# A graph network on one core: target look-ups, both moves of the edge order and its high digit placed inside the attention stages

## The reference, cut to what matters

```python
h = jnp.maximum(_layernorm(x, axis=-1), 0.0)
x = x + _L0_gnn_ref(h, edge_index, edge_attr_16, ...)      # two gat_conv layers
h = jnp.maximum(_layernorm(x, axis=-1), 0.0)
x = x + _L1_gnn_ref(h, edge_weight, src, dst, 3)           # three hops over the edges
h = jnp.maximum(_layernorm(x, axis=-1), 0.0)
x = x + _L2_gnn_ref(h, edge_index, edge_attr_64, ...)      # messages
h = jnp.maximum(_layernorm(x, axis=-1), 0.0)
x = x + _L3_gnn_ref(h, edge_index, ...)                    # three convolution layers

def gat_conv(x, src, dst, edge_attr, W, ...):
    xh = (x @ W).reshape(N, H, C)                          # H = 4 heads of C = 32
    alpha = leaky_relu(a_src[src_f] + a_dst[dst_f] + a_edge, 0.2)
    p = jnp.exp(alpha - segment_max(alpha, dst_f)[dst_f])
    alpha = p / (segment_sum(p, dst_f)[dst_f] + 1e-16)
    return segment_sum(xh[src_f] * alpha[..., None], dst_f).reshape(N, H * C) + bias
```

## Time and profile before

| | us |
|---|---|
| three runs | 8554.72, 8569.4, 8579.12 |
| median of these | 8569.4 |
| the profiled execution, whole | 8508.76 |
| its span, first to last instruction | 8507.1 |
| mean granted TensorE clock, share of full | 0.699 |

### The profile page before, as it was taken

The page is one execution under the profiler, slowest core; times in us unless marked ns, Lnnn a source line. Parts: engine busy times, 40 slices in busy tenths (PEclk is TensorE's granted clock), DMA queues, the critical chain, the costliest instruction groups (busy, mean ns, idle before and its releaser), DMA issues. The chain is left out here.

```text
span 8507.1 us, 77896 instructions
## 1 busy us (share of the span) xinstructions
PE 3708.8 (44%) x17298; PEld 2510.9 (30%) x17298; DVE 4381.7 (52%) x16544; ACT 2807.7 (33%) x6612; POOL 3976.6 (47%) x4025
## 2 busy tenths in 40 slices
PE   1501116711133452000676767466657889333333
PEld 1300004401022441000343434344434555223222
DVE  6340007906041741478888979567653445444322
ACT  3800006700031221012566656344433555222111
POOL 0047771062737026334534344466655442566566
PEclk9755558955565666555788889788777778666665
DMA  1000004521033253165334333344332332555433
GB/s 46 3 18 15 17 17 156 191 92 41 15 100 91 78 212 90 27 229 185 95 92 98 98 90 99 120 145 145 136 105 79 99 98 91 182 172 174 132 107 94
DMA packets 463932, 866.81 MB, mean 102 GB/s; under 512 B 110119, under 2 KB 119700, under 8 KB 461932
## 3 DMA queue, kind: packets, MB, share of 16 engines
q1 hardware_dynamic: 349035, 681.67, 23.2%
q0 software_dynamic: 114560, 181.50, 9.5%
HBM read 415.76 MB, written 459.09 MB: 103 GB/s over the span
## 5 line engine op out<-in xcount | busy, mean ns | idle before, releaser
L2756 POOL DMA_INDIRECT gcn_ring<-GT,gcn_index x588 | 590.8, 1005 | 255.0 <-issue 171.3
L1605 POOL DMA_INDIRECT light_ring<-C,light_s_u x392 | 392.2, 1001 | 402.8 <-DVE light_acc L1648 297.5
L1499 PE MATMUL tail_psT<-ident,tail_h 128*128 128x128 f32 x784 | 142.5, 311 | 724.5 <-ACT tail_h L1448 671.5
L2857 DVE SCALAR_TENSOR_TENSOR gcn_acc<-gcn_acc,cont,gcn_ring 128x128 f32<-128x128 f32 x588 | 204.7, 348 | 371.6 <-DMA gcn_ring<-GT,gcn_index 133.8
L532 POOL DMA_INDIRECT got_s<-TAB,src_u x196 | 185.8, 948 | 429.5 <-POOLq L560 366.0
L2366 POOL DMA_INDIRECT msg_ps<-PS,msg_s_u x196 | 189.8, 969 | 354.8 <-PE msg_ps_z L2662 298.1
L1499 PEld LDWEIGHTS tail_psT<-ident,tail_h 128*128 128x128 f32 x784 | 101.2, 155 | 857.3 <-ACT tail_h L1448 750.7
L2939 PE MATMUL gcn_psA<-ident,gcn_h 128*128 128x128 f32 x588 | 132.1, 365 | 498.0 <-DVE gcn_h L2860 253.1
L1448 ACT ACTIVATE tail_h<-tail_x,tail_nmr,tail_std 128x128 f32<-128x128 f32 x784 | 320.6, 483 | 14.4 <-DVE tail_nmr L1379 7.3
L2906 ACT ACTIVATE gcn_hT<-gcn_psA 128x512 f32<-128x512 f32 x147 | 88.6, 603 | 638.4 <-DMA X3D<-msg_x 245.9
L539 POOL DMA_INDIRECT J<-sort_items,sort_place x196 | 191.1, 975 | 199.1 <-POOLq L1714 137.0
(11 more groups left out here) (615 smaller groups left out, 14266.2 us busy)
## 6 DMA issues: line engine op xcount, KB each, us to landing
T<-front_a_t SPq DMA_DIRECT2D x160, 272.0 KB
source_rows_c<-C SPq DMA_DIRECT2D x156, 256.0 KB
GT<-source_rows_r SPq DMA_DIRECT2D x156, 256.0 KB
C<-light_acc SPq DMA_DIRECT2D x147, 256.0 KB
gcn_own<-GT SPq DMA_DIRECT2D x147, 256.0 KB
RC<-gcn_own SPq DMA_DIRECT2D x147, 256.0 KB
gat_rows_r<-RG SPq DMA_DIRECT2D x104, 264.0 KB
RG<-gat_rows SPq DMA_DIRECT2D x2, 12936.0 KB
```

Of the source, the lines that this page charges most:

```text
L1499: last = nc.tensor.transpose(ps["T"][:, j * P:(j + 1) * P], rows_[:, j, :], net.ident[:, :])
L1605: nc.gpsimd.indirect_dma_start(out=ring[:, n % RING, j, :], out_offset=None, in_=tables[h], in_offset=bass.IndirectOffsetOnAxis(ap=index[: ...
L2756: nc.gpsimd.indirect_dma_start(out=ring[:, n % RING, j, :], out_offset=None, in_=net.GT[i], in_offset=bass.IndirectOffsetOnAxis(ap=index[: ...
L2857: nc.vector.scalar_tensor_tensor(out=acc[:, n % 2, j, :], in0=before, scalar=net.cont[:, c:c + 1], in1=ring[:, n % RING, j, :], op0=ALU.mu ...
```

## The change

What GpSimd does beside the front is cut up and laid beside other phases:

- The front is one block of 98 groups. GpSimd beside it fetches the target rows (`fetch_target_rows`: 196 gathers in 14 batches; GpSimd itself issues the store of each batch to XD, one batch later, and waits for a store's landing before it fills that half of the ring again) and then makes the 196 look-ups `got_s`.
- The T1 rows are gathered by source straight into Y, 196 DMAs with no ring, no waits and no copies. Y is 136 wide now, and the store to RG takes the first 132 of each row.
- The attention stage of layer 1 gets, ahead of `fix_pool`, two casts of `got_s` and the first 150 `got_d` look-ups.
- `phase_gat1_rows` gets the other 46 look-ups, the 196 scatters into J1 and the load of the items; `gat_own` goes from GpSimd to DVE.
- `phase_high_digit` follows with 28 half batches instead of 14, and GpSimd gathers T2 beside it, straight into the second Y.
- The attention stage of layer 2 has no gather and no copies; GpSimd makes 100 of the scatters into J2 there.
- In `phase_gat2_rows` GpSimd's stream is written out; after each of the first 12 iterations it issues 8 of the remaining 96 scatters, after the last one the load. The two short phases on source segments come after it.

```diff
+def fetch_target_rows(nc, net, pool, table, index, ring, arrived, stored):
+    rows = net.XD.rearrange("(p t) d -> p t d", t=T)
+    def store(k):
+        pool.wait_ge(arrived[k % 2], 16 * U * (k // 2 + 1))
+        pool.dma_start(rows[:, k * U:(k + 1) * U, :], ring[:, k % 2, :, :]).then_inc(stored[k % 2], 16)
+    for k in range(NB):
+        if k >= 2:
+            pool.wait_ge(stored[k % 2], 16 * (k // 2))
+        for u in range(U):
+            c = k * U + u
+            nc.gpsimd.indirect_dma_start(out=ring[:, k % 2, u, :], out_offset=None, in_=table,
+                                         in_offset=bass.IndirectOffsetOnAxis(ap=index[:, c:c + 1], axis=0)).then_inc(arrived[k % 2], 16)
+        if k >= 1:
+            store(k - 1)
+    store(NB - 1)
+    for half in range(2):
+        pool.wait_ge(stored[half], 16 * (NB // 2))
...
+            def fetch_and_look_up(pool):
+                fetch_target_rows(nc, net, pool, inp["x"], dst_u, xd_ring, xd_arrived, xd_stored)
+                gather_static(nc, net.TAB, src_u, got_s, looked_s)
+                pool.wait_ge(looked_s, 16 * T)
+            phase_front(nc, net, inp, "front", 0, NODE_GROUPS, fetch_and_look_up)
...
+            Y = sb("gat1_rows", [P, T, WA])
+            def fetch_sources(pool):
+                gather_static(nc, net.T1, src_u, Y, rows1_in)
+                pool.wait_ge(rows1_in, 16 * T)
+            phase_own_projection(nc, net, fetch_sources)
+            def look_up(pool):
+                nc.gpsimd.tensor_copy(packed[:, :, 3], got_s[:, :, 0]).then_inc(filled, 1)
+                nc.gpsimd.tensor_copy(q_u[:, :], got_s[:, :, 0]).then_inc(filled, 1)
+                gather_static(nc, net.TAB, dst_u, got_d, looked_d, range(LOOKUPS_BEFORE_ENDS))
+            phase_attend(nc, net, 0, Y, look_up)
         def look_up_and_move(pool):
-            gather_static(nc, net.TAB, src_u, got_s, looked_s)
-            gather_static(nc, net.TAB, dst_u, got_d, looked_d)
-            pool.wait_ge(looked_s, 16 * T)
-            nc.gpsimd.tensor_copy(packed[:, :, 3], got_s[:, :, 0]).then_inc(filled, 1)
+            gather_static(nc, net.TAB, dst_u, got_d, looked_d, range(LOOKUPS_BEFORE_ENDS, T))
             pool.wait_ge(looked_d, 16 * T)
             nc.gpsimd.tensor_copy(packed[:, :, 4], got_d[:, :, 1]).then_inc(filled, 1)
-            pool.wait_ge(filled, 2)
+            pool.wait_ge(filled, 3)
             scatter_static(nc, net.J1, place, packed, moved)
...
-        phase_front(nc, net, inp, "front_a", 0, FRONT_BESIDE_LOOKUPS, look_up_and_move)
+        phase_gat1_rows(nc, net, look_up_and_move)
...
-            phase_high_digit(nc, net, items, place, lambda pool: gather_columns(nc, pool, inp["x"], net.dst_idx, xb), store_xd)
-        phase_front(nc, net, inp, "front_b", FRONT_BESIDE_LOOKUPS, NODE_GROUPS - FRONT_BESIDE_LOOKUPS, order_edges)
+            def fetch_rows(pool):
+                gather_static(nc, net.T2, q_u, Y, rows2_in)
+                pool.wait_ge(rows2_in, 16 * T)
+            phase_high_digit(nc, net, items, place, fetch_rows)
+            phase_attend(nc, net, 1, Y, lambda pool: scatter_static(nc, net.J2, place, items, moved2, range(MOVES_BEFORE_ENDS)))
+        def move(pool, it):
+            each = -(-(T - MOVES_BEFORE_ENDS) // EDGE_ITERS)
+            scatter_static(nc, net.J2, place, items, moved2, range(MOVES_BEFORE_ENDS + it * each, min(MOVES_BEFORE_ENDS + (it + 1) * each, T)))
+            if it == EDGE_ITERS - 1:
+                pool.wait_ge(moved2, 16 * T)
+                pool.dma_start(packed[:, :, :], as_columns(net.J2)).then_inc(loaded2, 16)
+                pool.wait_ge(loaded2, 16)
+        phase_gat2_rows(nc, net, move)
+        phase_segments(nc, net, packed, got_s, got_d)
...
-                if layer == 1:
-                    gather_columns(nc, pool, net.T2, net.q, b)
+                before_ends(pool)
                 pool.wait_ge(out_done, 16)
                 fix_pool(nc, pool, fix, net.RG, net)
...
-                sp.dma_start(net.RG.rearrange("(p t) d -> p t d", t=T), Y[:, :, :]).then_inc(out_done, 16)
+                sp.dma_start(net.RG.rearrange("(p t) d -> p t d", t=T), Y[:, :, 0:W_]).then_inc(out_done, 16)
...
-def phase_gat1_rows(nc, net):
+def phase_gat1_rows(nc, net, on_pool):
...
             def _(v):
                 with v.Fori(0, c.iters) as it:
+                    gat_own(c, net, v, nc.vector.tensor_tensor, it)
                     gat_divide(c, net, v, it)
...
             def _(pool):
-                with pool.Fori(0, c.iters) as it:
-                    gat_own(c, net, pool, it)
+                for it in range(c.iters):
+                    gat_own(c, net, pool, nc.gpsimd.tensor_tensor, it)
                     each_group(c, pool, it, ["XHX", "h1_made"], lambda g: nc.gpsimd.tensor_tensor(
                         flat(f["o"][g]), flat(f["x2"][g]), flat(f["h1"][g]), ALU.add), "x2_made")
+                    on_pool(pool, it)
```

More of the change, by code:

```diff
@@ L412, in allocate @@
     net.EA64 = dram("EA64", (EP, KE64))
[L420 to L451, removed]
 def owner_scan(nc, link, net, values, out):
@@ L470, in owner_carry @@
     link(last)
[L473 to L497, removed]
 def phase_own_rows(nc, net):
@@ L553, with phase_tables @@
 JUNK = 4
-def phase_tables(nc, net, key, packed, place, src_u, dst_u, got_s, got_d):
+def phase_tables(nc, net, packed, place, src_u, dst_u):
     with nc.cleanup_on_exit():
@@ L763, in _ @@
             def _(pe):
-                for k in range(NB):
+                for k in range(T // HU):
                     pe.wait_ge(made, k + 1)
                     for weight, ps in ((net.above, above_ps), (net.ones_b, total_ps)):
-                        for u in range(U):
-                            last = nc.tensor.matmul(ps[:, 0:R], weight[:, :], onehot[:, k % 2, u, :], start=k == 0 and u == 0, stop=k == NB - 1 and u == U - 1)
+                        for u in range(HU):
+                            last = nc.tensor.matmul(ps[:, 0:R], weight[:, :], onehot[:, k % 2, u, :], start=k == 0 and u == 0, stop=k == T // HU - 1 and u == HU - 1)
                     last.then_inc(freed, 1)
@@ L1734, in phase_index, with phase_segments @@
+        phase_gat2_rows(nc, net, move)
+        phase_segments(nc, net, packed, got_s, got_d)
+def phase_segments(nc, net, packed, got_s, got_d):
+    s_ = net.S
+    with nc.cleanup_on_exit():
+        sb = lambda name, shape, dt=F32: nc.alloc_sbuf_tensor(name, shape, dt)
+        tmp, ordered, got = sb("so_tmp", [P, 3, T]), sb("ordered", [P, 5, T]), sb("own_src_got", [P, 3, T], I32)
         with nc.cleanup_on_exit():
@@ L1861, in _ @@
             def _(pool):
-                fetch_columns(nc, pool, net.T1, net.src, b, lambda batch, half: nc.gpsimd.tensor_copy(
-                    Y[:, bass.ds(batch * U, U), :], b["ring"][:, half, :, 0:D + H]))
+                fetch(pool)
             @block.sync
@@ L1953, in _ @@
                 link(nc.vector.scalar_tensor_tensor(out=own[:, :, :], in0=own[:, :, :], scalar=NEG_SLOPE, in1=own[:, :, :], op0=ALU.mult, op1=ALU.max))
-                if layer == 1:
-                    with v.Fori(0, NB // 2) as k:
-                        for half in range(2):
-                            v.wait_ge(b["arrived"][half], k * (16 * U) + 16 * U)
-                            nc.vector.tensor_copy(Y[:, bass.ds((k * 2 + half) * U, U), :], b["ring"][:, half, :, 0:W_]).then_inc(b["freed"][half], 1)
-                    for half in range(2):
-                        v.wait_ge(b["freed"][half], NB // 2)
                 scores_in = Y[:, :, D:W_].rearrange("p t h -> p h t")
@@ L2037, in gat_divide, with gat_own @@
         heads(f["r"][g]), heads(f["r"][g]), f["inv"][g][:, :, :].unsqueeze(3).to_broadcast([P, S, H, CH]), ALU.mult), "gat_made")
-def gat_own(c, net, pool, it):
+def gat_own(c, net, engine, add, it):
     nc, f = c.nc, c.buf
@@ L2044, in gat_own @@
     heads = lambda buf: buf[:, :, 0:D].rearrange("p s (h c) -> p s h c", h=H)
-    each_group(c, pool, it, ["xh"], lambda g: nc.gpsimd.tensor_tensor(heads(f["xh"][g]), heads(f["xh"][g]), own(g).unsqueeze(3).to_broadcast([P, S, H, CH]), ALU.mult), "self_made")
-def phase_gat1_rows(nc, net):
+    each_group(c, engine, it, ["xh"], lambda g: add(heads(f["xh"][g]), heads(f["xh"][g]), own(g).unsqueeze(3).to_broadcast([P, S, H, CH]), ALU.mult), "self_made")
+def phase_gat1_rows(nc, net, on_pool):
     w = net.w
@@ L2972, in gnn_kernel @@
     phase_own_rows(nc, net)
[L2973 to L2977 removed]
+    phase_edges_and_attention(nc, net, inp)
     phase_light_and_tail(nc, net, out)
```

85 lines of the change are left out of this document (30 added, 55 removed).

## The result

The changed kernel took 8328.3 us (median of four, 8294.7 to 8331.4) against 8574.3 for the kernel before (8554.7 to 8613.9): 246 us less, ratio 0.970 with an interval of 0.966 to 0.974. The profiled execution took 8330.3 us, span 8328.6. So it got faster, by 71% of the 344 us forecast.

A forecast was written before the change was run, and what follows sets the result against it. GpSimd's back-to-back indirect DMAs were taken to bound the stages and delay neighbours' instructions. Stages 900 + 380 + 285 + 455 + 395 + 250 + 465 + 17 = 3147 against 3491, 344 less: 8569.4 - 344 = 8225 us, range 7950 to 8470.

The forecast's parts named there:

- choke: Beside GpSimd's back-to-back indirect DMAs other engines' instructions start late, on DVE one each 1.40 us; it ends soon after pauses.
- three signs of being wrong: First 335 us like old 508 to 756; scans 0.55 us apart beside look-ups; layer 1's loop under four iterations.
- Front: 98 groups beside target rows and got_s: 40 pass beside target rows, 6 beside got_s; 900 us (778 to 1087).
- Own projection: Beside 196 gathers of some 257 us, 4.6 iterations run and 8.4 follow: 380 us (365 to 432).
- second rival: No relief (0.18): store pauses too short, 5 front groups pass, 8412 us; 8522 if loops fall to the front's pace.
- Rows of layer 1: GpSimd's row 336 us with 5.7 iterations beside it, 6.5 remaining at 15.4 us: 455 us (430 to 513).
- High digit: Gather falls from 270 to 257 us, TensorE's catching up and places stay 137: 395 us (380 to 405).
- Attention, layer 1: 150 look-ups take 210 us, DVE slowed beside them, scored at 231, store 45, mending 10: 285 us (220 to 310).
- first rival: More relief (0.20): pauses keep the target-row fetch open, front 778, and DVE's scans are not slowed: 7964 us.
- Attention, layer 2: 100 scatters take 136 us, DVE slowed beside them, scored at 195, store 45, mending 10: 250 us (176 to 270).
- Rows of layer 2: DVE is the bound; eight scatters in each of twelve iterations add 131 us: 465 us (400 to 490).
- rival on the slower side: Slower (0.05): in layer 2's rows the slowdown outlives the 24 us between scatter bursts: 9070 us; gain gone from 62 an iteration.

The follow-up runs named there:

- e9: The changed kernel as it is, run again: 8235.7 us against 8500.1 for the kernel before, ratio 0.969.
- e10: The kernel before, unchanged, profiled again in a group where it took 8500: 8497.1 us.
- e2: Changed kernel plus a GpSimd wait for landing after every eighth DMA beside front, own projection, rows of layer 1 and high digit: 7819.5 us, ratio 0.908 to before.
- e4: Changed kernel plus 400 one-column memsets on DVE in the attention stage of layer 1, ahead of the scans: 8536.9 us.
- e7: Changed kernel plus a wait for landing after every sixteenth GpSimd DMA, none inside target-row batches: 6994.5 us, in a group where before took 7248.

## Why the prediction was right, and where it was off

The direction and the range held, and so did the main mechanism: GpSimd's rows set the stages they stand in, the rest comes from what runs beside them. The choke's price on the single stages did not hold. Of the prediction's three signs of being wrong two came: the scans started 0.46 us apart beside look-ups (132 in 60.4 us), and the loop of layer 1 made 1.8 iterations beside GpSimd's row (149 matmuls of 84 each), fewer than four. The sum was 344 and the stages gave 275 (272 by the table's cuts), 283 in e9 and e10. The medians differ by 246 and the two profiled executions by 178; what is missing to 275 lies behind the hops' first gather, in the part taken as unchanged, and how much of it the change costs stays open (97 us in the first pair, 15 in e9 and e10). Step by step:

- **Front, 50 us too low.** 27 node groups passed beside the target rows, not 40 (645 matmuls at 24 a group). The pause was taken for 7 us; the row says 3.6, which is the 21.5 us from store to store less 14 gathers:

```profile
587.36 0.58 POOL L488 DMA_DIRECT2D XD<-xd_ring  x1
591.61 0.97 POOL L494 DMA_INDIRECT xd_ring<-in_x,dst_u  x1 [3.67 <-DMA XD<-xd_ring]
```

  Shorter pauses, fewer open microseconds: 27 x 5.4 of 308 us are 47%, against the 69% assumed. The 3 us from the pause's start to the choke's end had no row behind it: the earlier trace rows have 6, and there DVE was waiting for a DMA of its own, so they don't show when a choke ends. GpSimd was done earlier, 559 us instead of 585, which gave part back. Beside got_s 6 groups were forecast and 6 passed (142 / 24).
- **Own projection, 66 too low.** The mis-sized term is the pace of 0.70 us a matmul, read beside the old gather. That row was broken by 14 copies on GpSimd, 2.7 us each without a DMA; without them it was 251 / 125 = 2.0 us, and with waits put in (e2) 291 / 729 = 0.40. Taking the copies away took the pauses away, which the second rival had as its further condition ("if the loops fall to the front's pace as well"); there it was 52, here 66. TensorE in the straight row, where a matmul and its weight load take turns, two instructions in 2.80 us, so 1.40 us each:

```profile
1553.15 0.37 PE L917 MATMUL own_projection_psB<-w_W,own_projection_hT 128*128 128x128 f32 x1 [2.43 <-issue]
1555.95 0.37 PE L917 MATMUL own_projection_psB<-w_W,own_projection_hT 128*128 128x128 f32 x1 [2.43 <-issue]
```

- **Rows of layer 1, 35 too low,** by the same term: 149 matmuls beside 321 us, 2.15 us each; 11.2 iterations were left, not 6.5.
- **High digit, 16 too low.** The gather was 4 us shorter than forecast; TensorE had 243 of 392 matmuls left when it ended.
- **Attention, layer 1, 56 too high.** Two terms were off, and neither sets the end in the trace. Scored at 2024 - 1903 = 121 us, as without look-ups, not 231: the step "32 instructions open, then one in 1.40 us" took the choke for a price on every instruction, and e4 shows that it is one on those not yet handed out. The store took 74 us, not 45, and still ended before the look-ups, which alone set the end: 150 in 217 us, 1.44 each. Up to 1960 it was 33 in 55 us, 1.67 each, and 1.93 apart beside DVE's multiplications of two large inputs (L1965); beside the scans 46 in 64 us, 1.39 each; later 1.25 with one gap of 9.15 us. So the 1.71 that the prediction drew from the rule on two SBUF inputs was passed for a stretch and not reached over the row, 217 us instead of 257. That the scans kept their pace was the first rival's word on this stage, 220 us, and it was right.
- **Attention, layer 2, 36 too high:** scored at 121 instead of 195, the store 77 instead of 45 on the path that sets the end. The first rival had the 121, but with the store at 45 its 176 us were 38 too low. The bounds given (31 to 60) had been too narrow; the nearer row was the gathers', not the whole store's.
- **Rows of layer 2, right:** 465 forecast, 467. DVE waits for GpSimd's own rows 129.9 us, 131 forecast, and the choke did not begin in bursts of eight (DVE busy for 311.4 us, as before). The line of DVE that waits:

```profile
L2003 DVE TENSOR_TENSOR gat_rows_r<-gat_rows_r,gat_rows_xh 128x512 f32<-128x512 f32 x52 | 69.9, 1402 | 129.9 <-POOL gat_rows_xh L2013 129.9
```

  The rival on the slower side had its point of decision at 62 us an iteration; it was 36.

The rival of no relief was wrong for the target rows and right for the loops; the rival of more relief was wrong for the target rows too and right for the scans. The errors of single stages add up to 167 us one way (50, 66, 35 and 16) and 92 the other (56 and 36); that the total missed by only some 100 us is in part luck, not method. The Trainium skill's sentence that PE never waits on anyone ("SBUF — State Buffer", "Who interferes with whom") stands in a section on SBUF ports. The rows of 2.43 us here show TensorE waiting beside GpSimd's row, in e7's group it didn't; whether the choke has to do with ports no run shows.

## What to carry to other kernels

Beside an unbroken row of indirect DMAs look at how far apart the neighbours' short instructions start, and not at how long they take; where they start 1.4 us apart, waiting for a landing every eight DMAs bought some 500 us here for 1.7 us a wait. A neighbour with few instructions for its time (the attention's 198 in 121 us) kept its own pace beside such a row, though GpSimd's row grew, to 1.44 us a look-up; a neighbour with many short ones (400 memsets) didn't. A pace read beside one kind of row doesn't carry over to another: take away the copies that broke it and the neighbour loses its openings. And time the kernel before again beside every experiment, since the same pauses cost up to 2% where nothing chokes.

## What the runs showed of the hardware

- The choke is there at some times and not at others, for the same program: before took 8500 and 8603 us in two groups, 7248 and 7253 in two. Its mark is one instruction in 1.40 us (sometimes 0.70) on TensorE and DVE alike, whatever the DMAs move: 8-byte look-ups, 20-byte scatters, 544-byte rows. By the record the 8500 and the 7253 both come from chip number 6, so the number of the chip alone doesn't decide it; what does isn't known.
- It sets in some 10 us after a row begins and lasts until some 15 us after its end in e4 (2108.5 to 2124); by the matmuls that pass, a wait of 1.7 us for a landing opens some 5 of 11.7 us, one of 3.6 us about 10 of 21.5.
- A store of 528-byte pieces out of 544 from SBUF took 74 and 77 us for 12,936 KB, 173 to 177 GB/s at a full DMA share, against 31 us and 427 GB/s in one run a partition (37 us beside scatters).
